# Attention with narrow causal masks, and both transposes of a pair's sums placed together

## The chip, the cores and the metric

The kernel runs on one core of one Trainium2 chip. The metric is the device time of one execution in microseconds. The kernel before has a median of 3471.86 us over three runs (3468.96 to 3472.17).

## The reference, cut to what matters

The reference is four layers in a row, each with a layer norm before and after and a residual sum: differential attention, a ternary feed-forward layer, a gated convolution layer and a mixture of experts. The change touches the attention alone:

```python
B, S, E = 8, 1024, 256; H, d = 16, 16
s1 = einsum('bhqd,bhkd->bhqk', q1, k1) / sqrt(d)      # two maps per head
s2 = einsum('bhqd,bhkd->bhqk', q2, k2) / sqrt(d)
a1, a2 = softmax(where(causal, s1, -inf)), softmax(where(causal, s2, -inf))
out = einsum('bhqk,bhkv->bhqv', a1 - lam * a2, v)     # v has 32 columns
out = (out - mean) / sqrt(var + eps) * (1 - LAM_INIT) # then merged @ Wo
```

The softmax needs the maximum of every query's row over the keys up to the query itself.

## The kernel before

The attention works on 64 pairs of heads, one pair after the other. A pair has two heads `a` and two maps `mp`, so four score matrices of 1024 by 1024, cut into eight query tiles of 128 and two key halves of 512.

**Two passes.** For a pair, TensorE first makes the scores with the queries on the partitions, only to find the row maxima. These go to a ring of four PSUM banks (`ring`, `NB = 4`). VectorE reads each bank with a maximum reduction and frees it (`ring_read`). Two pairs later TensorE makes the scores again, keys on the partitions, with the maxima folded into the product as three more rows (`scores`, tile `st`, three banks). ScalarE takes the exponentials (`att_p`), GpSimd zeroes the triangle of the diagonal tiles (`affine_select`, L909), and TensorE multiplies by the values (`pv`). ScalarE copies the sums of each query half out of PSUM (`copy_o`, L827), TensorE transposes them into the ring (`turn_sums`, L771), VectorE divides them (`norm`, L954 to L957), and GpSimd adds the two maps and scales by the root mean square (`add_up`, `scale`, L864 to L884).

**Column tiles.** All products of the attention are issued as four matmuls on four column tiles of TensorE, 32 stationary columns each (`in_tiles`, L743, and L790 for `pv`). Such four are called a group below. The transposes of the sums (L771) use the whole array. One transpose per pair of the maxima (`max_rows`, L763) uses 32 of its rows' outputs.

**Masks.** A maxima item on the diagonal (`diag` in `max_item`) of width `w` = 128, 256, 384 or 512 is a group over the `w` keys and then a group of 128 columns: the identity times `mask`, which adds -1e30 above the diagonal to the last 128 columns. Each score matrix has two such tiles of each width, so a pair has 32 of them, 24 of them wider than 128.

**Order.** TensorE follows an order written out by hand. A pair's turn has 48 slots, one for each `scores` group. `RING` is the order of the 41 things that go through the ring in one turn: 38 maxima items (of the pair two ahead), the transpose of the maxima of the next pair (`rows`), and two transposes of sums (`turn`). `RING_AT` gives the slot behind which each is issued; a number of 48 or more means the next turn. `PV_AT` and `COPY_AT` do so for the value products and the two copies. In the kernel before, `turn 1` of the previous pair stands behind `rows` in slot 27, and `turn 0` of a pair in slot 54, which is slot 6 of the next turn. VectorE goes through the ring in the order of `RING`. A ring step `k` waits until step `k - 4` is read:

```python
pe.wait_ge(ring_read, k - NB + 1)
```

and `norm` waits for the ring_read of the `norm` before it, as both use `rl`. GpSimd's order in a turn is: sums of the pair before last and of the last pair ahead of the first of the eight diagonal triangles, another `scale` ahead of the third (`SCALE_AT = 2`), the split of the maxima (`max_parts`) ahead of the fourth. After the last turn GpSimd serves two reciprocal roots for the feed-forward stage (`between`, L1003) and then finishes the sums that are left; the third root comes behind these. VectorE works in order too, and the step that waits for the third root (L1272) stands ahead of `x_low(0)` (L1290), on whose output TensorE's first feed-forward products wait.

Of the kernel before, what the change touches and what calls it, by code (L numbers as in the profile page):

```python
# [15 lines left out]
P = 128  # L16
# [3 lines left out]
VC = VD  # L20
# [3 lines left out]
GN = GT * P  # L24
# [583 lines left out]
def attend(nc, keep, first, I, C, parts, values, heads):  # L608
# [7 lines left out]
    KR = len(PARTS6) * D  # L616
    SL = 4
    T = B * H // 2
# [3 lines left out]
    R, NB, NS = 6, 4, 3  # L622
# [17 lines left out]
    NM = 4 * SB  # L640

    RING = [("max", n) for n in range(NI)]
    for before, step in ((2, ("rows", 0)), (3, ("turn", 1)), (27, ("turn", 0))):
        RING.insert(before, step)
    RING_AT = [23, 24, 27, 27, 29, 29, 29, 31, 32, 34, 34, 34, 34, 36, 37, 37, 39, 42, 42, 45, 46, 46, 48, 49,
               51, 51, 53, 54, 55, 55, 58, 59, 60, 61, 62, 63, 66, 66, 67, 67, 68]
    PV_AT = [9, 16, 21, 24, 30, 34, 36, 37, 40, 43, 50, 53]
    COPY_AT = [37, 54]
    SCALE_AT, PARTS_AT = 2, 3

    def ring_step(t, k):

        kind, n = RING[k]
        pair = {"max": t + 2, "rows": t + 1, "turn": t - n}[kind]
        return (kind, pair, n) if 0 <= pair < T and (kind, t) != ("rows", -1) else None

    RING_NO = {}
# [8 lines left out]
    with ExitStack() as ctx:  # L666
# [13 lines left out]
        ring = [m.ps(f"ring{i}") for i in range(NB)]  # L680
# [58 lines left out]
        def tensor(pe):  # L739
            def in_tiles(out, stationary, moving, start=True, stop=True):  # L740
# [2 lines left out]
                    ins = nc.tensor.matmul(out[row:row + VC], stationary[:, row:row + VC], moving, start=start, stop=stop, tile_position=(0, row))  # L743
                return ins

            def max_item(t, n):
                a, item = ITEMS[n]
                k, s = RING_NO["max", t, n], t % SL
                if k >= NB:
                    pe.wait_ge(ring_read, k - NB + 1)  # L750
                for x, (mp, i, c) in enumerate(item):
                    w, diag = min(GN, (i + 1) * P - c * GN), i // HB == c
                    ins = in_tiles(ring[k % NB][:, x * w:(x + 1) * w], ops[s][0:KR, a, mp, i * P:(i + 1) * P],
                                   ops[s][0:KR, a, 2 + mp, c * GN:c * GN + w], stop=not diag)
                    if diag:
                        ins = in_tiles(ring[k % NB][:, (x + 1) * w - P:(x + 1) * w], C["identb"][:], C["mask"][:], start=False)
                ins.then_inc(ring_ready, 1)
# [85 lines left out]
        def gpsimd(pool, between):  # L843
            done = Chain(pool, summed)
            steps, mc = Chain(pool, scaled), Chain(pool, mp_steps, 3)

            def max_parts(t):

                mc.turn(t)
                pool.wait_ge(ring_read, RING_NO["rows", t, 0] + 1)  # L850
                if t:
                    pool.wait_ge(max_placed[(t - 1) % SL], PLACED * ((t - 1) // SL + 1))
                mc.link(pool.tensor_copy(mpart[:, 0], mneg[:, 0]))
                mc.link(pool.tensor_tensor(mneg[:, 1], mneg[:, 0], mpart[:, 0], ALU.subtract))
                mc.link(pool.tensor_copy(mpart[:, 1], mneg[:, 1]))
                pool.tensor_tensor(mpart[:, 2], mneg[:, 1], mpart[:, 1], ALU.subtract).then_inc(mp_ready, 1)

            def add_up(t, x):

                k = 2 * t + x  # L860
                pool.wait_ge(ring_read, RING_NO["turn", t, x] + 1)
                both = o12[:, k % 2].rearrange("p b (a m) w -> p a b m w", a=2)
                for a in range(2):
                    pool.tensor_tensor(od[:, 0, a, :, 0:VR], both[:, a, :, 0], both[:, a, :, 1], ALU.add).then_inc(joined, 1)  # L864
                pool.wait_ge(joined, 2 * k + 2)
                done.link(pool.tensor_tensor(od[:, 1, :, :, 0:VR], od[:, 0, :, :, 0:VR], od[:, 0, :, :, 0:VR], ALU.mult))
                done.mark(pool.tensor_copy(osum[:, :, :, :, VR // 2:], od[:, :, :, :, VR // 2:VR // 2 + 1]))
                done.link(pool.tensor_tensor(osum[:, :, :, :, 0:VR // 2], od[:, :, :, :, 0:VR // 2], od[:, :, :, :, VR // 2 + 1:VR], ALU.add))
                for w in (8, 4, 2, 1):
                    done.link(pool.tensor_tensor(osum[:, :, :, :, 0:w], osum[:, :, :, :, 0:w], osum[:, :, :, :, w:2 * w], ALU.add))  # L870

            def scale(t, x):

                k, q, half = 2 * t + x, t % 2, 1 - x
                if t >= 2:
                    pool.wait_ge(o_stored[q], 16 * GB * (t // 2))
                total, square = osum[:, 0, :, :, 0], osum[:, 1, :, :, 0]
                keep = 1.0 / (1.0 - LAM_INIT) ** 2
                steps.mark(pool.tensor_scalar(od[:, 0, :, :, VR], total, -1.0, None, ALU.mult))
                steps.link(pool.tensor_tensor(orms[:], total, total, ALU.mult))  # L880
                steps.link(pool.tensor_tensor(orms[:], orms[:], square, ALU.add))
                steps.link(pool.tensor_scalar(orms[:], orms[:], keep / VD, keep * EPS, ALU.mult, ALU.add))
                steps.link(pool.tensor_tensor(orms[:], orms[:], C["neghalf"][:, 0:2 * HB].rearrange("p (a b) -> p a b", a=2), ALU.pow))  # L883
                pool.tensor_tensor(ofin[:, q, half * HB:(half + 1) * HB].rearrange("p b a v -> p a b v"), od[:, 0], bcast(orms[:].unsqueeze(3), [P, 2, HB, VD]),  # L884
                                   ALU.mult).then_inc(head_ready, 1)
                pool.wait_ge(head_ready, k + 1)

            pool.wait_ge(ones_set, 1)
            pool.memset(ops_more[KR:KR + 3, :, :, 2:4, :].rearrange("p s a m n -> p (s a) (m n)"), 1.0).then_inc(ones_set, 1)
            pool.wait_ge(ones_set, 2)  # L890
            max_parts(0)
            for t in range(T + 2):
                if t == T + 1:
                    between()
                for n, g in enumerate(DIAG):
                    if n == 0 and t >= 2:
                        add_up(t - 2, 1)
                        scale(t - 2, 1)
                    if n == 0 and 1 <= t <= T:
                        add_up(t - 1, 0)  # L900
                    if n == SCALE_AT and 1 <= t <= T:
                        scale(t - 1, 0)
                    if n == PARTS_AT and t + 1 < T:
                        max_parts(t + 1)
                    if t < T:
                        off = GROUPS[g][2]
                        pool.wait_ge(exp_done, t * NST + 4 * g + 4)
                        d = pr[:, g % R, :, off:off + P]
                        pool.affine_select(out=d, in_=d, compare_op=ALU.is_ge, fill=0.0, base=0,  # L909
                                           pattern=[[0, 4], [1, P]], channel_multiplier=-1).then_inc(masked, 1)  # L910
# [1632 lines left out]
```

## Time and profile before

| | |
|---|---|
| median of three runs | 3471.86 us (3468.96 to 3472.17) |
| the profiled execution | 3472.03 us, span 3470.3 us |
| mean granted TensorE clock over the span | 0.96 |
| busy over the span: PE, DVE, ACT, POOL | 3177.1, 2699.3, 2333.4, 1788.3 us |
| busy in the stretch 1200 to 1300 us: PE, DVE, ACT, POOL | 100.00, 92.35, 78.89, 72.01 us |

The profile is one execution. Its own time is 1.7 us more than its span. Busy time is a union: matmuls that overlap are counted once, and the start of an instruction is measured while the end of a matmul is modelled, so the distance from one start to the next tells more of TensorE than the durations. PE is the matmuls, PEld the weight loads, DVE is VectorE, ACT is ScalarE, POOL is GpSimd.

### The profile page before, as it was taken

The numbers are of one execution on the slowest core, as the hardware profiler recorded it, in microseconds if no ns is written. First come the engines' busy times: TensorE is split into PE (matmuls) and PEld (weight loads), VectorE is DVE, ScalarE is ACT, GpSimd is POOL, SyncE is SP. The second block draws the span as 40 slices with busy tenths as digits, with TensorE's granted clock in tenths as the row PEclk, the third lists the DMA queues.
The fourth block names the chain that finished last, engine by engine and source line by source line (L and its number), as shares of the span: only waits on it lengthen the run. The fifth ranks groups of instructions, "written<-read, shape, count | busy, mean of one in ns | idle before, by whom it ended". The sixth has DMA issues, their size and how long they took to land. (4 is left out here: it accounts for less than half of the span.)

```text
span 3470.3 us, 116948 instructions
## 1 busy us (share of the span) xinstructions
PE 3177.1 (92%) x46878; PEld 2150.8 (62%) x46878; DVE 2699.3 (78%) x5989; ACT 2333.4 (67%) x4989; POOL 1788.3 (52%) x3252
## 2 busy tenths in 40 slices
PE   8989899999999999999999998999998959969960
PEld 6766455555555555555555555888877746648850
DVE  7867899999999999999999972666655538845558
ACT  5655587778787788778887775777755546625533
POOL 1441377777777777777777774111101015647761
PEclk9999899999999999999999999999999979989985
DMA  7797533333333333333333312222251133336667
GB/s 240 238 262 235 89 85 82 85 77 81 82 84 84 77 82 83 85 82 78 81 86 84 80 36 96 92 78 82 66 166 50 61 103 104 118 130 189 195 196 268
DMA packets 380534, 396.79 MB, mean 114 GB/s; under 512 B 121368, under 2 KB 294424, under 8 KB 377816
## 3 DMA queue, kind: packets, MB, share of 16 engines
q1 hardware_dynamic: 366264, 351.46, 36.5%
q0 software_dynamic: 13728, 37.83, 3.0%
q8 instruction: 373, 6.11, 0.8%
q14 instruction: 169, 1.38, 0.1%
HBM read 230.29 MB, written 157.25 MB: 112 GB/s over the span
## 5 line engine op out<-in xcount | busy, mean ns | idle before, releaser
L837 ACT ACTIVATE att_p<-att_st 128x512 f32<-128x512 f32 (+3 forms) x3072 | 1328.3, 492 | 389.5 <-PE att_st L743 358.9
L923 DVE TENSOR_REDUCE att_mcol<-att_ring 128x1 f32<-128x512 f32 (+1 forms) x2048 | 1233.5, 649 | 124.3 <-PE att_ring L743 116.5
L743 PE MATMUL att_st<-att_ops_more 99*32 99x512 bf16 (+3 forms) x9216 | 679.2, 327 | 6.0 <-DMA att_ops_more<-att_mpart 4.1
L743 PE MATMUL att_ring<-att_ops_more 96*32 96x512 bf16 (+3 forms) x9216 | 650.4, 328 | 2.0 <-DMA att_va_more<-values 1.2
L909 POOL TENSOR_SCALAR_AFFINE_SELECT att_p<-att_p 128x512 f32<-128x512 f32 x512 | 325.5, 636 | 372.0 <-ACT att_p L837 362.9
L790 PE MATMUL att_pv<-att_p,att_va_more 128*32 128x512 f32 (+3 forms) x4608 | 474.8, 485 | 4.3 <-POOL att_p L909 2.4
L743 PEld LDWEIGHTS att_st<-att_ops_more 99*32 99x32 bf16 x9216 | 246.7, 97 | 293.0 <-ACT att_p L837 110.5
L743 PE MATMUL att_ring<-c_mask,c_identb 128*32 128x128 bf16 x8192 | 413.9, 221 | 0.0
L743 PEld LDWEIGHTS att_ring<-att_ops_more 96*32 96x32 bf16 x9216 | 252.4, 97 | 133.2 <-issue 40.4
L743 PEld LDWEIGHTS att_ring<-c_mask,c_identb 128*32 128x32 bf16 x8192 | 228.3, 98 | 82.1 <-issue 14.5
L743 PE MATMUL att_st<-att_ops 99*32 99x512 bf16 (+3 forms) x3072 | 230.8, 328 | 6.8 <-DMA att_ops<-att_mpart 6.7
L1003 POOL TENSOR_TENSOR ffn_rstd<-ffn_var,c_neghalf 128x4 f32<-128x4 f32 x48 | 48.4, 1008 | 358.9 <-DVE ffn_var L1268 358.8
L743 PE MATMUL att_ring<-att_ops 96*32 96x512 bf16 (+3 forms) x3072 | 221.0, 333 | 3.6 <-DVE att_mcol L923 2.2
L883 POOL TENSOR_TENSOR att_orms<-att_orms,c_neghalf 128x8 f32<-128x8 f32 x128 | 213.4, 1667 | 10.7
L2053 POOL DMA_INDIRECT moe_outs<-moe_work,moe_ident_u x158 | 164.9, 1044 | 57.9 <-issue 22.5
L790 PEld LDWEIGHTS att_pv<-att_p,att_va_more 128*32 128x32 f32 x4608 | 137.8, 110 | 74.3 <-ACT att_p L837 4.7
L870 POOL TENSOR_TENSOR att_osum<-att_osum 128x128 f32<-128x128 f32 (+3 forms) x512 | 158.5, 310 | 40.1
L925 DVE TENSOR_REDUCE att_mcol<-att_ring 128x2 f32<-128x512 f32 x256 | 174.3, 681 | 1.0 <-PE att_ring L743 1.0
L2031 POOL DMA_INDIRECT moe_rows<-moe_work,moe_slot x128 | 124.9, 976 | 74.3 <-DVE moe_slot L2336 38.6
L1003 POOL TENSOR_TENSOR cnv_rstd<-cnv_var,c_neghalf 128x8 f32<-128x8 f32 x16 | 27.1, 1694 | 263.5 <-DVE cnv_var L1753 263.5
L790 PE MATMUL att_pv<-att_p,att_va 128*32 128x512 f32 (+3 forms) x1536 | 158.9, 485 | 0.0
L2158 PE MATMUL moe_b<-moe_work 128*128 128x256 f32 x632 | 152.4, 384 | 0.7 <-issue 0.2
(299 smaller groups left out, 6659.5 us busy)
## 6 DMA issues: line engine op xcount, KB each, us to landing
att_ops_more<-parts SPq DMA_DIRECT2D x1152, 64.0 KB, 3.0
parts<-prj_pt SPq DMA_DIRECT2D x128, 384.0 KB, 3.2
att_ops<-parts SPq DMA_DIRECT2D x384, 64.0 KB, 2.9
moe_work<-moe_rows SPq DMA_DIRECT2D x79, 261.0 KB
values<-prj_vs SPq DMA_DIRECT2D x16, 1024.0 KB, 6.7
heads<-att_ofin SPq DMA_DIRECT2D x128, 128.0 KB, 2.7
ffn_os<-heads SPq DMA_DIRECT2D x16, 1024.0 KB, 4.9
moe_work<-x SPq DMA_DIRECT2D x32, 512.0 KB, 4.3
```

The costliest lines, as they stand in the source:

```text
L743: ins = nc.tensor.matmul(out[row:row + VC], stationary[:, row:row + VC], moving, start=start, stop=stop, tile_position=(0, row))
L790: ins = nc.tensor.matmul(op[row:row + VC, off:GN], va[t % SL][:, a, j, :], pr[:, g % R, b, off:GN], start=(j == 0), stop=(j == HB * (half ...
L837: act.activation(pr[:, g % R, b, off:GN], stp[(t * NST + n) % NS][:, off:GN], ACT.Exp, scale=SCALE).then_inc(exp_done, 1)
L870: done.link(pool.tensor_tensor(osum[:, :, :, :, 0:w], osum[:, :, :, :, 0:w], osum[:, :, :, :, w:2 * w], ALU.add))
L883: steps.link(pool.tensor_tensor(orms[:], orms[:], C["neghalf"][:, 0:2 * HB].rearrange("p (a b) -> p a b", a=2), ALU.pow))
L909: pool.affine_select(out=d, in_=d, compare_op=ALU.is_ge, fill=0.0, base=0, pattern=[[0, 4], [1, P]], channel_multiplier=-1).then_inc(maske ...
L923: ins = v.tensor_reduce(to[:, h, c, i % HB if c else i:(i % HB if c else i) + 1], of[:, 0:w], AX.X, ALU.max)
L925: ins = v.tensor_reduce(to[:, h, :, i], of[:, 0:2 * w].rearrange("p (c n) -> p c n", c=2), AX.X, ALU.max)
L1003: nc.gpsimd.tensor_tensor(rstd, var, self.C["neghalf"][:, 0:var.shape[1]], ALU.pow).then_inc(self.told, 1)
L2031: pool.indirect_dma_start(out=rows[:, :], out_offset=bass.IndirectOffsetOnAxis(ap=slot[:, g, n:n + 1], axis=0), in_=xn[:, g % XN, k, t], i ...
L2053: pool.indirect_dma_start(out=outs[:, :], out_offset=bass.IndirectOffsetOnAxis(ap=ident_u[:, i % XB, t:t + 1], axis=0), in_=yo[:, i % XB, ...
L2158: ins = nc.tensor.matmul(hx[i % 2][:, n * TT:(n + 1) * TT], wx[:, i % 2, n * W3 + c * P:n * W3 + (c + 1) * P], xgt[:, i % 2, c], start=(c ...
```

## The change

The maxima items on the diagonal that are wider than 128 are written differently. Each of the four column tiles holds 32 queries, and these need keys only up to their own. The group reads two ranges of `w/2` keys, the first from the start and the second ending at the last key that the 32 queries need; some keys are read twice, which does not alter a maximum. The mask then covers the last 32 columns instead of 128. The number of matmuls stays, as does the width of the first group.

In the order, both transposes of a pair's sums (`turn 0`, `turn 1` of the previous pair) are issued behind `rows` in slot 27, and no transpose stands in slot 54. GpSimd's `add_up` and `scale` of both halves move to the turn two after the pair.

```diff
     RING = [("max", n) for n in range(NI)]
-    for before, step in ((2, ("rows", 0)), (3, ("turn", 1)), (27, ("turn", 0))):
+    for before, step in ((2, ("rows", 0)), (3, ("turn", 0)), (4, ("turn", 1))):
         RING.insert(before, step)
-    RING_AT = [23, 24, 27, 27, 29, 29, 29, 31, 32, 34, 34, 34, 34, 36, 37, 37, 39, 42, 42, 45, 46, 46, 48, 49,
-               51, 51, 53, 54, 55, 55, 58, 59, 60, 61, 62, 63, 66, 66, 67, 67, 68]
+    RING_AT = [23, 24, 27, 27, 27, 29, 29, 29, 31, 32, 34, 34, 34, 34, 36, 37, 37, 39, 42, 42, 45, 46, 46, 48, 49,
+               51, 51, 53, 55, 55, 58, 59, 60, 61, 62, 63, 66, 66, 67, 67, 68]
...
-        pair = {"max": t + 2, "rows": t + 1, "turn": t - n}[kind]
+        pair = {"max": t + 2, "rows": t + 1, "turn": t - 1}[kind]
...
+            def up_to(keys, row, w):
+                return bass.AP(keys.tensor, keys.offset, (keys.ap[0], (w // 2 - P + VC + row, 2), (1, w // 2)))
...
                     w, diag = min(GN, (i + 1) * P - c * GN), i // HB == c
-                    ins = in_tiles(ring[k % NB][:, x * w:(x + 1) * w], ops[s][0:KR, a, mp, i * P:(i + 1) * P],
-                                   ops[s][0:KR, a, 2 + mp, c * GN:c * GN + w], stop=not diag)
+                    out, of, keys = ring[k % NB][:, x * w:(x + 1) * w], ops[s][0:KR, a, mp, i * P:(i + 1) * P], ops[s][0:KR, a, 2 + mp, c * GN:c * GN + w]
+                    if diag and w > P:
+                        for row in range(0, P, VC):
+                            nc.tensor.matmul(out[row:row + VC], of[:, row:row + VC], up_to(keys, row, w), start=True, stop=False, tile_position=(0, row))
+                        for row in range(0, P, VC):
+                            ins = nc.tensor.matmul(out[row:row + VC, w - VC:w], C["identb"][:, row:row + VC], C["mask"][:, row:row + VC],
+                                                   start=False, stop=True, tile_position=(0, row))
+                        continue
+                    ins = in_tiles(out, of, keys, stop=not diag)
                     if diag:
                         ins = in_tiles(ring[k % NB][:, (x + 1) * w - P:(x + 1) * w], C["identb"][:], C["mask"][:], start=False)
...
                 for n, g in enumerate(DIAG):
                     if n == 0 and t >= 2:
+                        add_up(t - 2, 0)
+                        scale(t - 2, 0)
                         add_up(t - 2, 1)
+                    if n == SCALE_AT and t >= 2:
                         scale(t - 2, 1)
-                    if n == 0 and 1 <= t <= T:
-                        add_up(t - 1, 0)
-                    if n == SCALE_AT and 1 <= t <= T:
-                        scale(t - 1, 0)
```

## Rows read from the trace of the kernel before

**Rows 1.** The page's first part: busy us, share of the span, instructions.
```profile
PE 3177.1 (92%) x46878; PEld 2150.8 (62%) x46878; DVE 2699.3 (78%) x5989; ACT 2333.4 (67%) x4989; POOL 1788.3 (52%) x3252
```
**Rows 2.** Busy time in windows: length, PE, PEld, DVE, ACT, POOL, granted clock, DMA.
```profile
1200.00:1300.00 100.00, 100.00 (x2294) 56.69 (x2284) 92.35 (x172) 78.89 (x187) 72.01 (x153) 1.00 0.32 78
```
**Rows 3.** One source line, 1000 to 1600 us: duration min/median/max, first and last start.
```profile
L763 PE MATMUL att_ring<-c_ident,att_mcol x22: 283/284/289, 1014.8 to 1582.4; 128*32 128x128 f32 x22
```
**Rows 4.** The page's costliest groups: the mask matmuls.
```profile
L743 PE MATMUL att_ring<-c_mask,c_identb 128*32 128x128 bf16 x8192 | 413.9, 221 | 0.0
```
**Rows 5.** Timeline of PE from slot 27 on: start us, us, what, count.
```profile
1203.59 0.60 PE L771 MATMUL att_ring<-c_ident,att_ot 128*128 128x128 f32 x4
1204.12 0.29 PE L743 MATMUL att_st<-att_ops_more 99*32 99x128 bf16 x8
...
1204.58 0.55 PE L743 MATMUL att_ring<-att_ops 96*32 96x512 bf16 x8
...
1205.02 0.23 PE L743 MATMUL att_st<-att_ops_more 99*32 99x128 bf16 x4
1205.08 1.03 PE L790 MATMUL att_pv<-att_p,att_va_more 128*32 128x512 f32 x8
1205.94 0.23 PE L743 MATMUL att_st<-att_ops_more 99*32 99x128 bf16 x4
1206.00 0.34 PE L743 MATMUL att_ring<-att_ops 96*32 96x384 bf16 x4
...
1206.44 0.40 PE L743 MATMUL att_ring<-att_ops 96*32 96x512 bf16 x4
...
1208.30 0.23 PE L743 MATMUL att_ring<-att_ops 96*32 96x128 bf16 x4
...
1208.78 0.39 PE L743 MATMUL att_ring<-att_ops 96*32 96x512 bf16 x4
```
**Rows 6.** Timeline of PE in the expert stage: matmuls of 16 columns.
```profile
2871.18 0.24 PE L2102 MATMUL moe_b<-moe_sel,moe_ones_b 128*128 128x16 bf16 x4
2871.28 1.53 PE L2092 MATMUL moe_b<-moe_work,c_sw 128*128 128x512 f32 x3
```
**Rows 7.** Timeline of PE around the other transpose of sums.
```profile
1191.18 0.41 PE L743 MATMUL att_st<-att_ops_more 99*32 99x512 bf16 x4
1191.52 0.66 PE L771 MATMUL att_ring<-c_ident,att_ot 128*128 128x128 f32 x4
```
**Rows 8.** Timeline of DVE in the stretch of rows 5.
```profile
1204.23 0.26 DVE L954 RECIPROCAL att_rl<-att_ring 128x16 f32<-128x16 f32 x1
...
1204.72 0.68 DVE L957 TENSOR_TENSOR att_o<-att_ring,att_rl 128x496 f32<-128x496 f32 x1
1205.31 0.68 DVE L925 TENSOR_REDUCE att_mcol<-att_ring 128x2 f32<-128x512 f32 x1
1205.91 3.63 DVE L923 TENSOR_REDUCE att_mcol<-att_ring 128x1 f32<-128x512 f32 x6
```
**Rows 9.** Timelines at 344 us, before the first exponentials, where PE waits for DVE.
```profile
343.68 1.14 DVE L923 TENSOR_REDUCE att_mcol<-att_ring 128x1 f32<-128x384 f32 x2
...
344.88 0.40 PE L743 MATMUL att_ring<-att_ops 96*32 96x512 bf16 x4 [0.20 <-DVE att_mcol L923]
```
**Rows 10.** Timeline of ACT around rows 7.
```profile
1188.52 3.89 ACT L837 ACTIVATE att_p<-att_st 128x512 f32<-128x512 f32 x7
...
1192.28 0.62 ACT L827 ACTIVATE att_ot<-att_pv 128x512 f32<-128x512 f32 x1
```
**Rows 11.** Timelines at the end of the attention, with idle time before and releaser.
```profile
2133.30 0.85 POOL L864 TENSOR_TENSOR att_od<-att_o 128x124 f32<-128x124 f32 x2
...
2140.92 1.01 POOL L1003 TENSOR_TENSOR ffn_rstd<-ffn_var,c_neghalf 128x4 f32<-128x4 f32 x1
2141.96 0.16 DVE L1272 SCALAR_TENSOR_TENSOR ffn_nmr<-ffn_mv,ffn_rstd 128x4 f32<-128x4 f32 x1 [2.89 <-POOL ffn_rstd L1003]
...
2142.87 1.94 PE L1130 MATMUL ffn_tp<-c_ident,ffn_os 128*128 128x128 f32 x8 [5.00 <-DVE ffn_xl L1290]
```

## The prediction

> **What bounds the kernel now.** I read the page first, to see which engine leads over the whole span: PE, with 3177.1 of 3470.3 us [rows 1]. A share over all stages says little, so I then read the windows of the attention. In each full window PE is busy all the time at a granted clock of 1.00, the 2.4 GHz level, DVE 92%, ACT 79%, POOL 72% [rows 2]. Since busy matmuls overlap, I checked by starts. Eight groups of 128 columns follow each other in 0.48 us, 0.060 us each [rows 5]. Two groups of 512 columns are 0.44 us apart from the start of the next work: a group costs about 0.42 ns a column and 5 ns on top. Counted so, a turn has 48 score groups and 48 maxima groups (18,432 columns each), 32 masks (4,096), 12 groups of value products (4,608 columns, each issued twice, at 0.43 us for 512) and nine transposes; that makes 26.8 us. The turn takes (1582.4 - 1014.8)/21 = 27.03 us [rows 3]. So PE streams without a pause, and its stream sets the time of 62 of the 64 turns (the last two have no maxima to make). The other engines have the rest as slack, and DVE's, 8%, is small. The order of the last instructions of the whole program says nothing here.
>
> **Masks.** 6 in 8 of the mask matmuls [rows 4] shrink from 128 to 32 columns: 24 groups in a turn. Now each takes 0.059 us (0.060 in rows 5, less rounding). No matmul of the attention is shorter than 128 columns, so the new price needs bounds. Below: 32 columns at 0.42 ns and 5 ns on top, 0.018 us. Above: 0.059 us, if the four weight loads behind each group, and not its columns, set the pace; a longer one is excluded, as the same loads stand in 0.060 us today. The nearest row is the expert stage's matmul of 16 columns, 4 starts in 0.10 us, 0.025 us each with a weight load of 128 columns each [rows 6]. I take 0.025: a saving of 24 x 0.034 = 0.80 us a turn.
>
> The Trainium skill, TensorEngine Tiling (Array Packing), Instruction Overhead, says that a matmul of one column takes as long as one of about 60, 60 cycles, which is 25 ns at 2.4 GHz; by that rule the sum is the same, and the trace agrees with its 0.025 us. The skill's page TensorE: Matmul & The Clock Gate, LDWEIGHTS, prices a weight load at its columns over 1.2 ns, 27 ns for 32 columns, and the tiling page says that column tiles have no fast load; by that, an estimate, a group would not go under 0.027 us and the sum would lose 0.05 us a turn. Four such loads in a row would be 107 ns, which rows 5 exclude.
>
> **Two ranges.** The wide groups stay as wide. New is that the four tiles read different keys. The value products already read four different operands and two groups of 512 take 0.86 us, 0.43 each, which is two passes at 0.42 ns a column [rows 5]. I take nothing. DVE reads banks of the same size as before, so it gains nothing from the narrow masks.
>
> **Transposes.** `turn 0` moves behind `rows` and `turn 1`. PE's own price for changing from column tiles to the whole array and back is visible: the group of 512 at 1191.18 should end its stream at 1191.40, the transposes start at 1191.52 [rows 7]; on the way out, four transposes at (0.60 - 0.27)/3 = 0.11 us end at 1204.03, and the next group starts at 1204.12 [rows 5]. 0.11 + 0.09 = 0.20 us a turn are saved, since one of two changes is gone.
>
> **What the ring then waits for.** This is the step against the change. DVE's work on one transposed half is long: from 1204.23 to 1205.40, with the next read 0.08 us before that end [rows 8]. Two of them now stand next to each other, while PE needs only 0.44 us more for the second. The ring has four banks, so the third, fourth and fifth item after the transposes wait for the first `norm`, the second, and the read behind it. Where PE waits for DVE it starts 0.06 us after the read's end (344.82 to 344.88) [rows 9]. By the times of rows 5 and 8:
> - Third item: 1204.80 today (the second of the x8), + 0.44 for the transposes, - 0.07 for two masks = 1205.17. The first `norm` ends at 1205.40, so it starts at 1205.45: 0.28 us of waiting.
> - The second `norm` waits for the first's end and ends at 1206.62. Fourth item: 1206.00 + 0.65 - 0.03 = 1206.62, allowed at 1206.68: 0.06 us.
> - The next read runs 1206.54 to 1207.22. Fifth item: 1206.44 + 0.68 - 0.03 = 1207.09, allowed at 1207.28: 0.19 us.
>
> Sum 0.53 us a turn. DVE is a little later afterwards, but it idles 8% of a turn [rows 2] and catches up there. Nothing is given back on PE where `turn 0` was: there DVE just waits longer.
>
> **ACT.** In slots 0 to 6 ACT makes seven exponentials in 3.89 us without a gap and then the copy [rows 10]. PE's 0.64 us around `turn 0` (0.44 and the change of tiles) lay there, and scores may run only three groups ahead of ACT. Part of the PE time gained there therefore turns into waiting for the exponentials. I take 0.10 us a turn, between nothing and 0.20.
>
> **POOL and DMA inside a turn** have the same work in the same slots (an `add_up`, a `scale` and an `add_up` ahead of the first triangle, a `scale` ahead of the third), fed earlier than they need. Nothing; the cover is that the sums were read from the ring a turn ago. If a triangle came late, `pv` on PE would wait.
>
> **The end of the attention.** POOL serves two roots, then finishes what is left. Before that was one half, 2133.30 to 2140.92, 7.6 us, and the third root followed at once; DVE had waited 2.89 us for it and PE 5.00 us behind DVE [rows 11]. Now two halves are left: the third root, DVE's `x_low(0)` and PE's first feed-forward products all come 7.6 us later. Nothing covers it; once.
>
> **Sum.** 0.80 + 0.20 - 0.53 - 0.10 = 0.37 us a turn, times 62 = 23 us gained, less 7.6 = 15 us. The profiled execution took 3472.03 us (span 3470.3), the median of runs is 3471.86: 3472 - 15 = 3457 us.
>
> **Rivals.**
> - A, the forecast: about 3457, between 3447 (0.018 us a mask) and 3465. Chance 0.48.
> - B, the ring wait is absent or small (DVE overlaps the two `norm`s, or the banks come free sooner): 0.80 + 0.20 - 0.10 = 0.90 us, 56 - 7.6 = 48 us, 3424. For it: many ring steps have slack; against it: the three sums above are direct readings. Chance 0.20.
> - C, slower: a mask group stays at 0.059 us because its weight loads set the pace. Without the 0.07 and 0.03 above the waits are 0.40 us, ACT's I put at 0.05: 0.20 - 0.40 - 0.05 = -0.25 us, 62 times that is 15 us lost, and 7.6: 3495. Four of the 24 masks lie ahead of a wait that takes their saving, so with a mask of p us the change breaks even where 20 x (0.059 - p) = 0.40 + 0.10 + 0.12 (the 7.6 us over 62 turns) - 0.20 = 0.42, p = 0.038 us. Chance 0.16.
> - D, the change does nothing measurable: a mask near 0.038 us, or ACT takes more. 3472. Chance 0.16.
>
> **How the numbers follow.** A measurement of this kernel tells some 0.2%, 7 us, from no change. Faster by more (under 3465): nearly all of A and B, 0.66. Within 3465 to 3479: D and a tail of A, 0.19. Slower: C, 0.15. The range reaches to B and towards C, 3425 to 3486; A's own is 3445 to 3467.
>
> **What would show it.** Mask groups of 32 columns 0.025 us apart in PE's timeline; one pair of changes around eight transposes in a row; PE idle about 0.5 us a turn in slots 29 to 32, released by DVE's L957 and L925; a turn of 26.66 us by L763; DVE busy above 93%; and the third root's start 15.2 us after POOL's first `add_up` behind `between`. Wrong if the masks stay 0.06 us apart, if the wide groups of two ranges take longer than 0.22 us, or if PE shows no wait behind the two `norm`s.

## The result and the profile after

The changed kernel takes 3481.19 us, the median of eight runs (3477.17 to 3487.6). The kernel before, run beside it, takes 3470.34 us (3466.46 to 3477.03). The ratio is 1.0031, 95% interval 1.0022 to 1.0040: slower by 0.3%. Forecast were 3457 us and a gain. The profiled execution of the changed kernel took 3487.6 us, the longest of its eight.

**Where the time went.** The stretch of the 63 turns is read from the line that transposes the maxima, here at its new number, over the whole program:

```profile
L774 PE MATMUL att_ring<-c_ident,att_mcol x64: 283/284/395, 362.3 to 2074.6; 128*32 128x128 f32 x64
```

From its first to its last start are 2074.6 - 362.3 = 1712.3 us. The same line of before ran from 357.1 to 2069.7, 1712.6 us. All the loss of about 11 us lies behind the last turn, and none of the gain promised for the turns has come. (The profiled execution, 15.6 us longer in span than that of before, was also 5.2 us late ahead of the first turn; the medians of the two kernels differ by 10.85 us.) Between 1000 and 1600 us:

```profile
L774 PE MATMUL att_ring<-c_ident,att_mcol x22: 283/284/287, 1019.4 to 1587.6; 128*32 128x128 f32 x22
```

That is 568.2/21 = 27.06 us a turn, against 27.03 [rows 3]. The page's rows of the groups with two ranges (three in four of them, in three widths: 256 columns and, as "+2 forms", 384 and 512) and of the narrowed masks, and the window that answers to [rows 2]:

```profile
L760 PE MATMUL att_ring<-att_ops_more 96*32 96x256 bf16 (+2 forms) x4608 | 349.1, 328 | 6.7 <-DVE att_o L967 1.2
L762 PE MATMUL att_ring<-c_mask,c_identb 128*32 128x32 bf16 x6144 | 287.0, 181 | 0.0
```

```profile
1200.00:1300.00 100.00, 99.26 (x2300) 54.60 (x2291) 91.45 (x172) 77.70 (x183) 73.29 (x153) 1.00 0.33 83
```

PE is no longer full, 99.26 us of 100, and since overlapping matmuls are counted once this hides most of its waiting. The granted clock is 1.00 as before. What PE waits for is seen in its timeline behind the transposes (start us, us, what, count), here with both `turn` transposes in the x8:

```profile
1208.69 1.04 PE L782 MATMUL att_ring<-c_ident,att_ot 128*128 128x128 f32 x8
1209.66 0.30 PE L743 MATMUL att_st<-att_ops_more 99*32 99x128 bf16 x8
1209.78 0.29 PE L760 MATMUL att_ring<-att_ops 96*32 96x256 bf16 x4
1209.89 0.19 PE L762 MATMUL att_ring<-c_mask,c_identb 128*32 128x32 bf16 x4
1209.92 0.28 PE L760 MATMUL att_ring<-att_ops 96*32 96x256 bf16 x4
1210.03 0.19 PE L762 MATMUL att_ring<-c_mask,c_identb 128*32 128x32 bf16 x4
1210.06 0.39 PE L743 MATMUL att_ring<-att_ops 96*32 96x512 bf16 x4
1210.55 0.35 PE L760 MATMUL att_ring<-att_ops 96*32 96x384 bf16 x4
...
1210.81 1.03 PE L801 MATMUL att_pv<-att_p,att_va_more 128*32 128x512 f32 x8
1211.67 0.23 PE L743 MATMUL att_st<-att_ops_more 99*32 99x128 bf16 x4
1211.85 0.35 PE L760 MATMUL att_ring<-att_ops 96*32 96x384 bf16 x4
1212.03 0.19 PE L762 MATMUL att_ring<-c_mask,c_identb 128*32 128x32 bf16 x4
1212.06 0.39 PE L743 MATMUL att_st<-att_ops_more 99*32 99x512 bf16 x4
1212.45 0.40 PE L743 MATMUL att_ring<-att_ops 96*32 96x512 bf16 x4
```

DVE in the same stretch:

```profile
1209.83 0.67 DVE L967 TENSOR_TENSOR att_o<-att_ring,att_rl 128x496 f32<-128x496 f32 x1
...
1211.12 0.67 DVE L967 TENSOR_TENSOR att_o<-att_ring,att_rl 128x496 f32<-128x496 f32 x1
1211.72 0.68 DVE L935 TENSOR_REDUCE att_mcol<-att_ring 128x2 f32<-128x512 f32 x1
```

A group of 512 columns gives way after 0.22 us (the one at 1210.06 to 1210.28), yet the third item starts at 1210.55, 0.05 us behind the end of the first `norm` (1209.83 + 0.67). The fourth starts at 1211.85, 0.06 us behind the second `norm`, and the fifth at 1212.45, 0.05 us behind the next read. Over 25 turns the mean idle ahead of the three is 0.275, 0.126 and 0.178 us, in sum 0.58 us. (These means, and those below, are the distances of starts less what a group of that width takes where nothing is waited for.) A mask group of 32 columns gives way after 0.03 us (1209.89 to 1209.92), and the groups with two ranges take as long as those with one did: over all turns a mean of 0.110, 0.166 and 0.217 us for 256, 384 and 512 columns, 0.112, 0.164 and 0.218 before.

The second place is slots 6 to 9, behind the slot that `turn 0` has left. ACT first, then PE:

```profile
1221.35 3.78 ACT L848 ACTIVATE att_p<-att_st 128x512 f32<-128x512 f32 x7 [0.16 <-PE att_st L743]
1225.01 0.62 ACT L838 ACTIVATE att_ot<-att_pv 128x512 f32<-128x512 f32 x1
1225.48 2.60 ACT L848 ACTIVATE att_p<-att_st 128x512 f32<-128x512 f32 x5
```

```profile
1223.05 0.62 PE L743 MATMUL att_st<-att_ops_more 99*32 99x512 bf16 x8
...
1223.89 0.71 PE L743 MATMUL att_st<-att_ops_more 99*32 99x512 bf16 x8
...
1224.90 0.69 PE L743 MATMUL att_st<-att_ops_more 99*32 99x512 bf16 x8
1225.67 1.06 PE L801 MATMUL att_pv<-att_p,att_va_more 128*32 128x512 f32 x8
```

From the first of these exponentials on, ACT has no gap. Two groups of scores without a wait are the x8 at 1223.05, 0.62 us; the two below it took 0.71 and 0.69 us, because the second group of each (slots 7 and 9) waited for an exponential to free its bank. Then `pv(0)` of the turn starts at 1225.67, right behind the end of ACT's copy (1225.01 + 0.62 = 1225.63): it writes the PSUM bank `op`, which the copy reads. The list of waits between 1000 and 1600 us shows the ring's and ACT's (us in total, times, longest; these are waits of PE's weight loads, PEld, and hold more than PE's own idle time):

```profile
PEld att_st L743 <- ACT att_p L848: 68.5, 258, 0.3
PEld att_ring L760 <- DVE att_o L967: 20.1, 44, 0.5
PEld att_pv L801 <- ACT att_ot L838: 8.5, 22, 0.4
```

The means over 25 turns are 0.094 us (slot 7), 0.070 us (slot 9) and 0.273 us (`pv(0)`), in sum 0.44 us of waiting for ACT. In before PE waits for nothing at these three places.

**The end of the attention**, with the rows that answer to [rows 11]:

```profile
2118.13 0.85 POOL L875 TENSOR_TENSOR att_od<-att_o 128x124 f32<-128x124 f32 x2
2119.07 0.26 DVE L964 RECIPROCAL att_rl<-att_ring 128x16 f32<-128x16 f32 x1 [6.16 <-POOL att_od L875]
2120.45 3.77 PE L1140 MATMUL ffn_tp<-c_ident,ffn_os 128*128 128x128 f32 x16 [7.96 <-DVE att_o L967]
...
2141.85 0.86 POOL L875 TENSOR_TENSOR att_od<-att_o 128x124 f32<-128x124 f32 x2
2149.45 0.85 POOL L875 TENSOR_TENSOR att_od<-att_o 128x124 f32<-128x124 f32 x2
2157.05 1.01 POOL L1013 TENSOR_TENSOR ffn_rstd<-ffn_var,c_neghalf 128x4 f32<-128x4 f32 x1
2158.10 0.16 DVE L1282 SCALAR_TENSOR_TENSOR ffn_nmr<-ffn_mv,ffn_rstd 128x4 f32<-128x4 f32 x1 [12.16 <-POOL ffn_rstd L1013]
2159.01 1.94 PE L1140 MATMUL ffn_tp<-c_ident,ffn_os 128*128 128x128 f32 x8 [13.43 <-DVE ffn_xl L1300]
```

Two halves, 2141.85 and 2149.45, stand ahead of the third root, which starts 15.20 us behind the first. PE waits 13.43 us there, where it waited 5.00 us before. From the last transpose of maxima to the third root are 2157.05 - 2074.6 = 82.45 us; before, 2140.92 - 2069.7 = 71.2 us. That is 11.2 us, more than the 7.6 us of one half. The rest lies at 2119.07: DVE's `norm` of the last half waits 6.16 us for POOL to have read the half before it, and PE's first transposes of the feed-forward stage wait behind that `norm`. In before, they waited 1.8 us. That this delay makes up the other 3.6 us is read from these rows alone; no run takes it away.

### The profile page after: what moved, and what is told of

Read it like the earlier page. It is cut to its first block and busy times, and to the rows that moved or that the text cites. A ratio compares the mean times of both kernels' runs of the same rounds, so it can differ in the third digit from the quotient of the medians.

```text
span 3485.9 us, 116948 instructions
## 1 busy us (share of the span) xinstructions
PE 3162.8 (91%) x46878; PEld 2103.4 (60%) x46878; DVE 2689.1 (77%) x5989; ACT 2314.3 (66%) x4989; POOL 1784.1 (51%) x3252
## 5 line engine op out<-in xcount | busy, mean ns | idle before, releaser
L848 ACT ACTIVATE att_p<-att_st 128x512 f32<-128x512 f32 (+3 forms) x3072 | 1313.3, 494 | 408.5 <-PE att_st L743 392.3
L933 DVE TENSOR_REDUCE att_mcol<-att_ring 128x1 f32<-128x512 f32 (+1 forms) x2048 | 1217.3, 647 | 133.4 <-PE att_ring L762 93.4
L743 PE MATMUL att_ring<-att_ops_more 96*32 96x512 bf16 (+1 forms) x4608 | 356.8, 328 | 2.7 <-DMA att_va_more<-values 1.9
L760 PE MATMUL att_ring<-att_ops_more 96*32 96x256 bf16 (+2 forms) x4608 | 349.1, 328 | 6.7 <-DVE att_o L967 1.2
L762 PE MATMUL att_ring<-c_mask,c_identb 128*32 128x32 bf16 x6144 | 287.0, 181 | 0.0
L762 PEld LDWEIGHTS att_ring<-c_mask,c_identb 128*32 128x32 bf16 x6144 | 172.5, 96 | 66.8 <-issue 15.0
L743 PEld LDWEIGHTS att_ring<-att_ops_more 96*32 96x32 bf16 x4608 | 127.8, 96 | 62.4 <-DVE att_mcol L935 15.3
```

Source lines behind the costliest of these rows:

```text
L760: nc.tensor.matmul(out[row:row + VC], of[:, row:row + VC], up_to(keys, row, w), start=True, stop=False, tile_position=(0, row))
L762: ins = nc.tensor.matmul(out[row:row + VC, w - VC:w], C["identb"][:, row:row + VC], C["mask"][:, row:row + VC], start=False, stop=True, ti ...
L848: act.activation(pr[:, g % R, b, off:GN], stp[(t * NST + n) % NS][:, off:GN], ACT.Exp, scale=SCALE).then_inc(exp_done, 1)
L933: ins = v.tensor_reduce(to[:, h, c, i % HB if c else i:(i % HB if c else i) + 1], of[:, 0:w], AX.X, ALU.max)
```

## The experiments

In each run `before` is the kernel before on the same chip. "Stretch" is the start of the last transpose of maxima less that of the first, 1712.6 us in before and 1712.3 in the changed kernel: all 63 turns without the work ahead and behind. What lies behind it, to the end of the program, is the tail: 1400.6 us in before, 1411.3 in the changed kernel.

### The two parts apart

**Masks alone**: `max_item` as changed, `RING`, `RING_AT` and GpSimd's order as before. **Order alone**: the reverse, with masks of 128 columns.

> The narrow masks with two key ranges alone, in the order of the kernel before (turn 0 in slot 54, GpSimd's order of before). Theory (the order costs what the masks give, through DVE's two norms in a row, ACT's slots 4 to 10 and the end of the attention): the mask groups stay about 0.029 us apart, so a turn is 24 x 0.034 = 0.8 us shorter less some waits for exponentials, 26.2 to 26.4 us, and the whole is 40 to 50 us faster than the kernel before, near 3425. Rival (ACT or DVE hold the turn near 27.0 us whatever PE does, so the narrow masks are worth nothing): within 7 us of 3470.

> The order alone: both transposes behind rows, GpSimd's add_up and scale two turns late, masks of 128 columns. Theory: one change of tiles saved, 0.26 us a turn; waits for the ring 0.45 us (without the masks PE arrives 0.1 us later), waits in slots 7 to 10 about 0.3 us; so 0.5 us a turn lost, 31 us, and 11 us at the end of the attention: 3505 to 3515. Rival (the order costs nothing in the turn, only the end's 11 us): 3465 to 3481.

Masks alone: 3441.33 us, ratio 0.9905 (0.9890 to 0.9920). Order alone: 3515.25 us, ratio 1.0134 (1.0120 to 1.0149). The stretches, masks alone above:

```profile
L774 PE MATMUL att_ring<-c_ident,att_mcol x64: 283/285/394, 357.9 to 2051.9; 128*32 128x128 f32 x64
```

```profile
L763 PE MATMUL att_ring<-c_ident,att_mcol x64: 283/284/286, 358.3 to 2104.3; 128*32 128x128 f32 x64
```

1694.0 and 1746.0 us. The order alone came out at the upper end of its theory, the masks alone 16 us above theirs. So the change is a gain and a loss: the masks gain, the order loses more than its transposes save. PE's three waits for ACT are not in masks alone, where `turn 0` stands in its old slot, and all three are in the order alone. With wide masks the three ring waits are 0.21, 0.09 and 0.15 us, a little less than 0.58 in sum because the groups between them are longer, and the copy's wait of 0.27 us is the same. The tail tells the same of the end: from 1393 to 1401 us in the seven profiled executions (before among them) whose order is that of before, from 1407 to 1413 us in the seven with the changed order.

The stretch of masks alone is 18.6 us shorter than that of before, where 62 turns at 0.80 us would make 49.6. Its waits between 1000 and 1600 us show where some of it is lost:

```profile
PEld att_st L743 <- DMA att_ops_more<-att_mpart: 10.9, 14, 2.2
PEld att_st L743 <- DMA att_ops<-att_mpart: 6.7, 4, 2.0
```

Turns of 26.2 us stand beside some of 28 us and more. With a shorter turn, the maxima sometimes come too late: GpSimd splits them (`mpart`), six DMAs place them, and the next turn's first scores need them. In one such turn PE waits 2.24 us. Between 400 and 2040 us these waits of PE alone come to 15.3 + 6.7 = 22.0 us, against 3.3 + 0.8 = 4.1 in before.

The waits have a second price. In before and in the changed kernel the granted clock of TensorE is 1.00 (2.4 GHz) from 400 to 2040 us. In masks alone it stands at 0.50 (1.2 GHz) in four pieces of that time, 17 us in all, which start at 775.1, 1123.3, 1608.0 and 1799.1 us: around and shortly behind the end of waits of 2.10, 1.70, 2.24 and 1.85 us for these DMAs. (Five more waits, of 1.5 to 1.9 us, had no such piece behind them.) At half the clock 17 us do the work of 8.5. With the 17.9 us of added waits that is 26 of the 31 us that are missing.

### The wait for the copy

**`pv(0)` one slot later** in the changed kernel, so that the copy is done when it comes:

```diff
-    PV_AT = [9, 16, 21, 24, 30, 34, 36, 37, 40, 43, 50, 53]
+    PV_AT = [10, 16, 21, 24, 30, 34, 36, 37, 40, 43, 50, 53]
```

> The changed kernel with the first value product of a pair one slot later (slot 10 in place of 9), so that PE comes to it about 0.2 us later than ACT's copy out of the same bank needs. Theory (PE's wait of 0.27 us in slot 9 is for the copy, which stands behind seven exponentials on ACT): the wait falls to under 0.1 us and the turn to 26.8 us, 10 to 15 us faster than the changed kernel, near 3468. Rival (ACT is the bound from slot 4 to 11, and the wait moves to the next score groups): no change, 3481.

3512.79 us, ratio 1.0126 (1.0112 to 1.0141), 32 us slower than the changed kernel and outside both the theory and the rival. The wait does not go, it becomes 0.76 us, ahead of the scores of slot 10. The product's 0.86 us had been PE's work while ACT caught up; without it PE has only scores to issue, and these may run three groups ahead of ACT. ACT is the limit of these slots, and the copy's wait is only where this becomes visible.

**The copy one slot earlier**:

```diff
-    COPY_AT = [37, 54]
+    COPY_AT = [37, 53]
```

> The changed kernel with ACT's second copy of the sums behind the exponential of slot 5 instead of slot 6 (COPY_AT = 37, 53). Theory (PE's 0.27 us in slot 9 is a wait for this copy, and the 0.16 us ahead of it are waits for exponentials behind the copy in ACT's order): the 0.27 us go, the others stay or grow by the rest of the copy, the turn is 26.8 to 26.9 us and the kernel 8 to 17 us faster than the changed one, 3464 to 3473. Rival (ACT is the bound throughout slots 4 to 11, so where the copy stands among the exponentials does not matter): 3481 within 5 us.

3495.7 us, ratio 1.0083 (1.0070 to 1.0096), 15 us slower than the changed kernel, another miss. The product's wait is gone, and in its place PE waits 0.56 us for the exponentials. In the turn below the copy stands one exponential earlier, and the scores wait for the exponential that is now behind it:

```profile
1225.84 0.60 ACT L838 ACTIVATE att_ot<-att_pv 128x512 f32<-128x512 f32 x1
1226.32 5.96 ACT L848 ACTIVATE att_p<-att_st 128x512 f32<-128x512 f32 x11
```

```profile
1226.99 0.40 PE L743 MATMUL att_st<-att_ops_more 99*32 99x512 bf16 x4 [0.39 <-ACT att_p L848]
1227.22 1.03 PE L801 MATMUL att_pv<-att_p,att_va_more 128*32 128x512 f32 x8
```

**Less work for ACT** instead of another place for it; half of this copy's columns are left out of the computation:

```diff
-                act.activation(ot[:, x], op[:], ACT.Copy).then_inc(o_copied, 1)
+                w = GN // 2 if x and t else GN
+                act.activation(ot[:, x, 0:w], op[:, 0:w], ACT.Copy).then_inc(o_copied, 1)
```

> The changed kernel, where ScalarE's second copy of a turn's sums (in slot 6) moves only 256 of its 512 columns in every turn but the first; the other columns of ot keep old values, so that the run leaves out a part of the sums. Theory (ScalarE is the limit of slots 4 to 9, and its copy there stalls the first product by 0.27 us and the scores of slots 8 and 9 by 0.16 us): ScalarE gets back about 0.25 us in those slots, the 0.27 us wait of the product in slot 9 is 0.05 or less, the turn goes from 27.06 to 26.8 us, time 3481 - 62 x 0.25 = 3465 us. Rival (the product waits for something else, or the gain is taken by the next wait, for the fourth scores or for the ring): turn 27.0 us, time 3476 to 3481.

3466.3 us, ratio 0.9995 (0.9986 to 1.0004), against 1.0031 for the changed kernel: 0.0036 of 3468, 12 us less. The stretch is 1699.7 us, 12.6 less, 0.20 us a turn. The product's wait went from 0.273 to 0.059 us; the two of 0.094 and 0.070 stayed, as they must, since they are for exponentials that ACT makes ahead of the copy. Of the expected 15.5 us 12 came. This shows the copy's term directly: 0.21 us of the turn went with half of the copy.

### The ring

**The second half's `norm` shortened** in the changed kernel:

```diff
-                nch.link(v.reciprocal(rl[:], o[:, :, :, VR]))
...
-                nch.link(v.tensor_tensor(rl[:, :, 1:4:2], rl[:, :, 1:4:2], bcast(lam.unsqueeze(1), [P, HB, 2]), ALU.mult))
+                if x == 0:
+                    nch.link(v.reciprocal(rl[:], o[:, :, :, VR]))
...
+                    nch.link(v.tensor_tensor(rl[:, :, 1:4:2], rl[:, :, 1:4:2], bcast(lam.unsqueeze(1), [P, HB, 2]), ALU.mult))
```

The second half uses the first one's reciprocals, so its own are left out of the computation.

> The changed kernel, but the second norm of a pair leaves out its reciprocal and its product with lambda and uses those of the first half; so VectorE's second transposed half takes 0.68 us and waits for nothing, where it took 1.17 us and waited for the first to end. This leaves part of the computation out. Theory (PE's waits of 0.28, 0.13 and 0.18 us in slots 29 to 32 are for VectorE's two norms): the first stays, the other two, 0.31 us, go; the turn is 26.75 us and the kernel 15 to 20 us faster than the changed one, near 3463. Rival (what PE gains there it waits for ACT in slots 7 to 10 instead): 3475 to 3481.

3462.06 us, ratio 0.9982 (0.9973 to 0.9991), 17 us less than the changed kernel by the ratios (0.0049 of 3470), stretch 1696.6 us, 15.7 less. The fourth and fifth items' waits, 0.126 and 0.178 us, are gone; the third's, which waits for the first `norm`, is still 0.275. So the 0.30 us of the two are real waits and no artefact of the reading. Of 62 x 0.30 = 19 us 16 came; the first scores of a turn wait some 6 us more in all for the DMAs of the maxima, which covers what is missing.

### The end of the attention

**Four roots ahead of the last sums** in the changed kernel, instead of two:

```diff
-    FIRST, LAST = 2, len(power_order()) - 2
+    FIRST, LAST = 4, len(power_order()) - 2
```

> The changed kernel with GpSimd serving four roots of the feed-forward stage, not two, before it finishes the last pair's sums. Nothing in the turns changes. Theory (the third root stands behind 15.2 us of sums, and DVE and PE behind it): the third root comes right after its variance, 11 us earlier; PE's wait of 13.4 us falls to about 3, and the kernel is 8 to 11 us faster than the changed kernel, 3470 to 3473. Rival (the heads of the last pair or the fifth root are late instead, and the time comes back): under 3 us.

3476.61 us, ratio 1.0020 (1.0011 to 1.0028). The waits of PE's L1140 between 2040 and 2270 us:

```profile
PE ffn_tp L1140 <- DVE att_o L967: 8.0, 1, 8.0
...
PE ffn_tp L1140 <- DMA ffn_os<-heads: 3.6, 1, 3.6
PE ffn_tp L1140 <- DVE ffn_xl L1300: 3.2, 1, 3.2
```

The wait of 13.4 us shrank to 3.2, but the last heads are now finished and stored later, and PE waits 3.6 us for their load. By the ratios 0.0011 of 3470, 4 us, is left of the 10 us, and the intervals of the two ratios overlap; the tail is 3.1 us shorter. The 8.0 us behind `norm` is untouched.

**The same with masks alone:**

> The narrow masks alone in the order of before, and four of GpSimd's roots of the next stage ahead of the last sums instead of two. Theory (at the end of attention the roots stand behind the sums on GpSimd; before and masks alone wait 5.0 us for them): 3 to 5 us less than masks alone, 3436 to 3439 us, if masks alone is again 3441. Rival: the two roots delay GpSimd's last sums and the DMAs of the last heads by 4 us, and the time is that of masks alone or above it, 3441 to 3447 us.

3433.29 us, ratio 0.9904 (0.9889 to 0.9919), the ratio of masks alone. Its stretch is 1679.2 us, with fewer of the DMA waits (11.5 us of PE's) and two pieces at the lower clock instead of four, so a gain of under 5 us in the end cannot be told from this run. Nothing is gained that can be measured.

### The DMA chain of masks alone

**GpSimd's `scale` and `max_parts` exchanged** in masks alone, so that the maxima are split one triangle earlier and the scale comes one later:

```diff
-    SCALE_AT, PARTS_AT = 2, 3
+    SCALE_AT, PARTS_AT = 3, 2
```

> The masks alone, in the order of before, with GpSimd's split of the maxima (max_parts) ahead of its scale instead of behind it (SCALE_AT, PARTS_AT = 3, 2). In the masks alone most turns are 26.2 to 26.4 us, but some are 28 to 31 us, where the first scores of a turn wait up to 2.2 us for the transfer of the split maxima. Theory (the chain scale, split, six transfers, landing has become the tight one, since PE is 0.75 us faster): with the split 3.4 us earlier the long turns go, all turns are 26.2 to 26.4 us, and the kernel is 10 to 15 us faster than the masks alone, near 3428; the scale stands ahead of the fourth triangle now, which may cost pv 0.3 us a turn of it. Rival (the late transfers come from the queue, not from GpSimd): as the masks alone, 3441.

3461.14 us, ratio 0.9983 (0.9975 to 0.9992): 27 us more than masks alone by the ratios (0.0078 of 3469), where 10 to 15 us less were expected. No DMA wait is among its waits between 1000 and 1600 us any more, but these are:

```profile
PEld att_pv L801 <- ACT att_p L848: 22.9, 22, 1.1
POOL att_mpart L864 <- DVE att_mneg L954: 20.8, 22, 0.9
```

GpSimd comes to `mpart` 0.95 us before VectorE has the maxima and stands still. Then the `scale` of 3.4 us comes ahead of the fourth triangle, and the product that reads this triangle (`pv` in slot 37) waits 0.8 us in each turn. GpSimd idles a quarter of a turn, but not there.

**Only `max_parts` moved**, ahead of the third triangle and behind the `scale`:

```diff
-    SCALE_AT, PARTS_AT = 2, 3
+    SCALE_AT, PARTS_AT = 2, 2
```

> The narrow masks alone in the order of before, and GpSimd's splitting of the maxima (mpart) ahead of the third triangle, behind the scale, instead of behind that triangle. Theory (with the masks narrowed, the chain GpSimd's mpart, then six DMAs, then the first scores of the next turn ends last in some of the turns, 59 us of such waits in all in the masks-alone run, counted for TensorE and its weight loads): the chain starts 0.6 us earlier, those waits fall under 15 us, the third triangle is 1.6 us later and no product waits for it; turns 26.2 us throughout, time 3415 to 3430 us. Rival (the third triangle's delay hits the product that reads it, as the delayed triangles did where the scale stood ahead of the fourth one): a wait of a product for GpSimd or ScalarE of 0.3 to 1 us in each turn, time 3445 to 3480 us. Third: the DMA waits come from the time that the transfers need, not from their start, and stay: 3438 to 3444 us.

3426.15 us (3419.67 to 3430.67), ratio 0.9885 (0.9870 to 0.9901). GpSimd's order in a turn, with the third triangle behind the split and run at once with the fourth:

```profile
1209.42 0.62 POOL L895 TENSOR_TENSOR att_ofin<-att_od,att_orms 128x256 f32<-128x256 f32 x1
1210.11 0.28 POOL L864 CAST att_mpart<-att_mneg 32x128 bf16<-32x128 f32 x1
...
1211.32 0.42 POOL L867 TENSOR_TENSOR att_mpart<-att_mneg,att_mpart 32x128 bf16<-32x128 f32 x1
1211.70 1.22 POOL L920 TENSOR_SCALAR_AFFINE_SELECT att_p<-att_p 128x512 f32<-128x512 f32 x2
```

```profile
L774 PE MATMUL att_ring<-c_ident,att_mcol x64: 283/286/394, 358.6 to 2021.4; 128*32 128x128 f32 x64
```

The stretch is 1662.8 us, 49.8 less than before, with only 0.4 us of PE's waits for these DMAs in it and the granted clock at 1.00 from 400 us on. The product that reads the third triangle (slot 36) waits 0.03 us a turn for it. Since the interval touched that of masks alone, both kernels ran once more, side by side:

> Masks alone once more, beside the kernel with the maxima split ahead of the third triangle, since their intervals so far overlap (0.9890 to 0.9920 and 0.9870 to 0.9901). Theory (the late DMAs of the maxima cost masks alone some 0.2 us a turn): ratio 0.989 to 0.992, and DMA waits again in its chain of waits.

> Masks alone with the maxima split ahead of the third triangle, once more, beside masks alone. Theory (its chain starts 0.6 us earlier and the DMA waits are nearly gone): ratio 0.987 to 0.990, 5 to 15 us less than masks alone in the same job. Rival (the difference seen was chance, and the DMA waits vary from execution to execution whatever the start): the two medians within 4 us, both profiles with DMA waits of the same size.

Masks alone: 3438.35 us, ratio 0.9914 (0.9899 to 0.9929), stretch 1673.4 us, PE's DMA waits 6.7 us. With the split ahead: 3422.92 us (3419.23 to 3424.86), ratio 0.9866 (0.9850 to 0.9881), stretch 1669.6 us, waits 5.2 us. The intervals are apart, 15 us lie between the medians, and this is the fastest kernel of the study, 1.3% faster than before. So the earlier split helps; but the sum of these waits differs so much from one execution to the next (22.0 and 6.7 us in one kernel, 0.4 and 5.2 in the other) that the two profiles of this pair don't show where its 15 us come from. Each of the two had one piece at the lower clock, behind a wait of 1.80 and of 1.85 us.

The traces also say which part of the chain is late. The first of the six DMAs is issued 0.03 us behind the end of the split in every turn. From there to the last landing it takes 5.7 us in the median turn of before and of masks alone (of the 30 turns there whose six landings the trace has), but 7.7 us ahead of the wait of 2.10 us. Before has two such turns (7.4 and 7.1 us), the kernel with the split ahead one of 8.1. So the long turns come from the issue and transfer of the DMAs, and an earlier split only gives these more room.

## Why the prediction was wrong

Its direction was wrong: 24 us too low, though inside its range. By its own steps:

- **Masks, 0.80 us a turn: right.** Measured are distances of 0.028 to 0.029 us from the start of a mask group to the next start, not 0.025, and 0.003 us less for the group that follows, so that PE's own stream is 24 x (0.030 + 0.003) = 0.79 us shorter. The stretches with the split ahead are 49.8 and 43.0 us shorter than that of before, 0.80 and 0.69 us a turn; what lacks in the second is of the size of its DMA waits and its piece at the lower clock. By the estimate that the prediction made from the Trainium skill's page TensorE: Matmul & The Clock Gate, LDWEIGHTS, a group would not go under 0.027 us; the rows agree with that bound. The 0.05 us that the sum would lose by it did not show, because of the 0.003 us of the groups behind.
- **Two ranges at nothing: right**, since the wide groups keep their times.
- **Transposes, 0.20 us: mis-sized, 0.26 us.** The way out of `turn 0` in slot 54 had cost 0.092 us as forecast, the way in 0.111, and between the first and the second of the four transposes lie another 0.055 us.
- **Ring waits, 0.28 + 0.06 + 0.19 us: mechanism and sum right**, 0.275 + 0.126 + 0.178 = 0.58 us, shown by the shortened `norm` for two of the three.
- **ACT, 0.10 us: this is the step that failed; it measures 0.44 us.** The prediction saw that PE's work at `turn 0` covered ACT and bounded the loss by 0.20, by scores alone. It did not ask for the copy itself: `pv(0)` in slot 9 needs the bank that the copy reads, and the copy in slot 6 is behind seven exponentials. With 0.64 us of PE's work gone ahead of them, PE arrives at `pv(0)` before the copy ends, with wide masks as with narrow ones. The part that the prediction named, scores behind exponentials, came to 0.16 us; the copy, which it put at nothing, to 0.27. The missing 0.34 us, times 62, are 21 of the 24 us. It is shown that the waits come with the move of `turn 0` (they are in the order alone and not in masks alone), that the copy's length sets the larger one, and that other places for the product or the copy make it worse.
- **The end, 7.6 us: mis-sized, 11.2 us.** One half more ahead of the third root was right, 15.20 us from the first `add_up` as forecast. Missing was the `norm` of the last half, which waits 6.2 us for POOL to read the half before it; that this makes the other 3.6 us is argued, not tested.

The sum with what was measured: 0.80 + 0.26 - 0.58 - 0.44 = 0.04 us gained a turn; in the 25 turns read, another 0.02 us went to the first scores of a turn, which waited 0.106 us before and 0.122 now, and 0.02 us to `pv(0)`, whose matmuls behind the wait are that much slower. That makes 0.00 us, where 27.03 and 27.06 us a turn were read, so 0.03 us stay unaccounted for. (Over all 62 turns the first scores waited 0.16 us in before and 0.12 now; the stretches differ by 0.3 us.) With 11.2 us at the end: 3470.3 + 11 = 3481 us.

**The rivals.** B is excluded, as the ring waits are there in full. C, the slower one, had its mask groups at 0.059 us, and they measure 0.029; that 3481 us lies in the stated range is owed to the room left for C, and so to luck. D named two ways to no gain, and its second, that ACT takes more, is what happened inside the turns. Of the signs listed, the turn of 26.66 us (27.06) and DVE above 93% (91.45) failed; the mask groups, the single pair of changes, the idle time in slots 29 to 32 and the third root's 15.2 us came, the mask groups at 0.029 us for 0.025.

The prices of the two parts do not add up exactly. Stretches: 43 to 50 us gained by the masks where the DMAs come in time, 33.4 lost by the order (1746.0 - 1712.6), would leave a gain of 10 to 16 us; measured is 0.3. Narrower masks give PE 0.8 us less work in a turn and so less cover: the waits for the ring and for ACT's exponentials in slots 7 and 9 are longer with them, 0.58 against 0.45 us and 0.16 against 0.10 us, or 62 x 0.19 = 12 us.

**Left open:** why the six DMAs of the maxima take up to 2.4 us longer in some turns, in before too; the median of one from issue to landing is 1.8 us. Not tried either: a second bank beside `op` for the products, and another place for `turn 0` that covers ACT and leaves room behind `turn 1`.

## What to carry to other kernels

Where an engine sets the pace and its order has been filled by hand, each piece of its work is also cover for the other engines: before moving a piece away, list every instruction of the others that ends within it, bank copies too, and ask what next needs them. Two consumers' worth of work on a ring with few banks should not be placed next to each other when the producer needs a third of the consumer's time for them. And a gain on the leading engine shortens the turn for all chains that run once in it; the next of them, here GpSimd's split and six small DMAs, took back about half of the gain in one execution, a third of that through the lower clock behind its waits, and less once it was started earlier.

## What the runs showed of the hardware

- Four column tiles of 32 stationary columns with 32 moving columns each, loads of weights among them, follow each other in 0.028 to 0.029 us, against 0.059 us with 128 columns. The loads did not set the pace at 128.
- A moving operand in two ranges, with another offset for each column tile, streams as one range does (0.22 us for 512 columns, 0.17 for 384, 0.11 for 256).
- A change of PE from column tiles to the whole array and back cost 0.11 us on the way in, 0.055 us behind the first transpose and 0.09 us on the way out; four more transposes next to four others cost none of it.
- Six DMAs of 4 KB, issued each turn in the same place, cost the same kernel 22.0 us of PE's waiting in one execution and 6.7 us in another.
- Behind four of the nine waits of TensorE of about 1.5 us and more in masks alone, its granted clock stood at 0.50 (1.2 GHz) for 17 us in all; in before, with two waits of 1.1 and 1.4 us, it stayed at 1.00.
